# Thresholds of small scores on GpSimd, and adjacency loads behind a unit's four thresholds

## The chip, the cores and the metric

The kernel runs on one core of a Trainium2 chip. The metric is the device time of one execution in microseconds; less is better. The engines are TensorE (PE in the profile; its weight loads are PEld), VectorE (DVE), ScalarE (ACT), GpSimd (POOL) and SyncE (SP), which here only issues DMA transfers. GpSimd issues transfers too. Each engine works through its own queue in order.

## The reference

x is 4096 x 512, adj is 4096 x 4096 with entries 0 and 1. One attention layer masked by adj, and one aggregation by adj, each with a residual sum and a layer norm:

```
q, k, v = x @ Wq.T + bq, key @ Wk.T + bk, value @ Wv.T + bv
s = (q @ k.T) / 64 * adj
s = where(abs(s) < 1e-5, -1e9, s)
x = layernorm(x + (softmax(s) @ v) @ Wm.T + bm)
out = layernorm(x + relu((adj @ x) @ W.T + b))
```

## The kernel before, in words

Weights, keys and values are split into a high and a low fp16 part, and each product is made as three (high by high, low by high, high by low). After a preparation, attention runs over 64 units. A unit g is a tile of 128 rows against one half of the 4096 keys: units 0 to 31 are the tiles against the first half, units 32 to 63 against the second. NT is 32, MC is 4; b is the parity of the tile and picks the buffer.

In a unit TensorE makes the scores in four chunks of 128 x 512, each in its own PSUM bank (L887), and at the end weighs the values with the transposed probabilities (L907). The order on TensorE is scores of g, then weigh of g - 1; in the second half a product of x1 (L942) and a projection (L928) stand between them.

For each chunk c of the scores:

- VectorE masks it: prob = (score + c_now) * adj, L1559, `masked`.
- ScalarE takes its magnitude into the tile small (two buffers, c % 2), L1204. For chunk c it waits for mask c and for the sum of chunk c - 2.
- VectorE makes of it the threshold, `small_scores`, L1565: -1e9 (scaled) where the magnitude is under the limit, 0 elsewhere; `small_ready` (L1569) waits for it.
- VectorE adds the threshold to prob and keeps the maximum, `threshold`, L1572. This is called the sum below.

After the four sums come the row's maximum (L1578, L1581), the exponential on ScalarE (L1209), the high part on ScalarE (L1217) and the low part on VectorE (L1588). SP transposes both parts by DMA into PT (L387, L390), and TensorE's weigh waits for both.

The adjacency half rows come as a converting load on GpSimd's queue into adjh (two buffers, `load_adj`, L714). The load of unit g waits for all masks of unit g - 2, and for the store of that tile as bf16 (`store_adj` on SP, L374). The 64 loads stand in two loops. Behind them on the same queue stand the loads of Y, the first product of the second layer (`load_y`, L731): chunks 0 and 1 at once after the loops, chunks 4 to 6 after the last probability transpose, then 2 and 3.

SP issues in a unit, in this order: the load of t (L360), the load of x, the adjacency store, the two transposes, and then stores and transposes of other results. In the last unit it issues before the two transposes six transposes of the stored adjacency into AT (L511), for the aggregation that follows. The aggregation (L1002, L1035) starts when the last weigh, one product of x1 and one projection are done, and reads Y chunks 0 and 1 first.

Of the kernel before, what the change touches and what calls it, by code (L numbers as in the profile page):

```python
# [9 lines left out]
ALU = mybir.AluOpType  # L10
# [33 lines left out]
def attention_then_aggregation(nc, x, adj, key, value, wq, bq, wk, bk, wv, bv, wm, bm, w1, b1, out):  # L44
# [3 lines left out]
    NT = N // P  # L48
# [3 lines left out]
    MC = HALF // C  # L52
# [32 lines left out]
    with ctx:  # L85
# [17 lines left out]
        eps_s = sb(ctx, "eps_s", [P, 1], fp32)  # L103
        neg_s = sb(ctx, "neg_s", [P, 1], fp32)
# [228 lines left out]
        with nc.Block() as block:  # L333
# [327 lines left out]
            def _(pool):  # L661
# [59 lines left out]
                load_adj(1, 1, 1, 0)  # L721
                with pool.Fori(1, NT // 2) as i:
                    for b in range(2):
                        load_adj(2 * i + b, b, 2 * i + b, 0)
                with pool.Fori(0, NT // 2) as i:
                    for b in range(2):
                        load_adj(2 * i + b, b, NT + 2 * i + b, 1)

# [648 lines left out]
            def _(dve):  # L1377
# [184 lines left out]

                def small_scores(g, b, c):
                    dve.wait_ge(s_abs, MC * g + c + 1)
                    nc.vector.tensor_scalar(small[:, c % 2, :], small[:, c % 2, :], eps_s[:, 0:1], neg_s[:, 0:1],  # L1565
                                            ALU.is_lt, ALU.mult).then_inc(s_neg, 1)

                def small_ready(g, c):
                    dve.wait_ge(s_neg, MC * g + c + 1)  # L1569
# [149 lines left out]
                def score_chunks(g, b, j, n=None):  # L1719

                    def inverse(step):
                        if n is not None and step < ROOT_STEPS - 1:
                            inverse_deviation(n, 1 - b, step)

                    if not isinstance(g, int) or g != 1:
# [3 lines left out]
                        inverse(1)  # L1729
                    small_scores(g, b, 0)  # L1730
                    inverse(2)
                    small_ready(g, 0)
                    masked(g, b, 2, j)
                    inverse(3)
                    threshold(b, 0)
                    inverse(4)
                    small_scores(g, b, 1)
                    inverse(5)
                    small_ready(g, 1)
                    masked(g, b, 3, j)  # L1740
                    inverse(6)
                    threshold(b, 1)
                    inverse(7)
                    small_scores(g, b, 2)
                    inverse(8)
                    small_ready(g, 2)
                    small_scores(g, b, 3)
                    inverse(9)
# [366 lines left out]
```

## Time and profile before

| | us |
|---|---|
| three runs | 2064.64, 2064.67, 2067.79 |
| their median | 2064.67 |
| the profiled execution | 2066.32 |
| its span, first to last instruction | 2064.6 |
| TensorE busy in the span | 2036.5 |
| VectorE busy | 1446.6 |
| ScalarE busy | 698.9 |
| GpSimd busy | 81.5 |

The profile is of one execution. The span is what its rows cover; the rest of that execution's own time, 1.7 us, lies around it. TensorE's granted clock is 0.996 of full over the span. A busy time adds up the instructions of an engine; it does not say what another engine waited for. All times of rows are microseconds from the start of the span unless they are marked ns.

### The profile page before, as it was taken

The numbers are of one execution on the slowest core, as the hardware profiler recorded it, in microseconds if no ns is written. First come the engines' busy times: TensorE is split into PE (matmuls) and PEld (weight loads), VectorE is DVE, ScalarE is ACT, GpSimd is POOL, SyncE is SP. The second block draws the span as 40 slices with busy tenths as digits, with TensorE's granted clock in tenths as the row PEclk, the third lists the DMA queues.
The fourth block names the chain that finished last, engine by engine and source line by source line (L and its number), as shares of the span: only waits on it lengthen the run. The fifth ranks groups of instructions, "written<-read, shape, count | busy, mean of one in ns | idle before, by whom it ended". The sixth has DMA issues, their size and how long they took to land.

```text
span 2064.6 us, 29824 instructions
## 1 busy us (share of the span) xinstructions
PE 2036.5 (99%) x9471; PEld 977.7 (47%) x9471; DVE 1446.6 (70%) x3339; ACT 698.9 (34%) x948; POOL 81.5 (4%) x139
## 2 busy tenths in 40 slices
PE   8899999999999999999999999999999999999998
PEld 7784444444444444444444444444444444444443
DVE  4767656565656665687777777778888758877887
ACT  4665443434343434343333333334443310000000
POOL 1110000000000000000000000000000000000000
PEclk9999999999999999999999999999999999999999
DMA  7777876766677676887766666777777897555551
GB/s 260 245 275 177 207 164 165 164 171 156 169 160 172 156 172 152 219 185 163 163 163 163 163 163 163 168 173 183 182 183 210 213 276 167 125 122 124 136 133 65
DMA packets 586675, 359.58 MB, mean 174 GB/s; under 512 B 501376, under 2 KB 505472, under 8 KB 586240
## 3 DMA queue, kind: packets, MB, share of 16 engines
q1 hardware_dynamic: 565056, 275.07, 53.2%
q0 software_dynamic: 21568, 83.89, 16.8%
q8 instruction: 24, 0.39, 0.1%
q14 instruction: 27, 0.22, 0.0%
HBM read 181.15 MB, written 88.60 MB: 131 GB/s over the span
## 4 chain that ended last, share of the span: by engine, by line
PE 95%; DVE 2%; DMA 1%; ACT 1%; SPq 0%; issue 0%; ACTq 0%; DVEq 0%
PE ps L907 32%; PE ps L887 31%; PE ps L1035 16%; PE ps L928 4%; PE ps L942 4%; PE ps L836 4%; PE ps L1002 3%; PE ps L791 1%; PE ps L820 1%; PE ps L783 0%; PE ps L774 0%; DMA t_in<-t_dram 0%; DMA stg<-in_L_gnn_value 0%; DVE V L1477 0%; PE ps L861 0%
## 5 line engine op out<-in xcount | busy, mean ns | idle before, releaser
L887 PE MATMUL ps<-KT,thl 128*128 128x512 f16 x3072 | 674.9, 380 | 2.5 <-DVE thl L1529 2.5
L907 PE MATMUL ps<-V,PT 128*128 128x512 f16 x3072 | 673.5, 379 | 3.0 <-DMA PT<-Phl 2.8
L887 PEld LDWEIGHTS ps<-KT,thl 128*128 128x128 f16 x3072 | 300.9, 98 | 366.2 <-DVE thl L1529 2.7
L907 PEld LDWEIGHTS ps<-V,PT 128*128 128x128 f16 x3072 | 300.4, 98 | 365.8 <-issue 4.0
L1559 DVE SCALAR_TENSOR_TENSOR prob<-ps,c_now,adjh 128x512 f32<-128x512 f32 x256 | 191.7, 750 | 271.5 <-PE ps L887 270.3
L1204 ACT ACTIVATE small<-prob 128x512 f32<-128x512 f32 x256 | 161.1, 630 | 616.7 <-DVE prob L1559 333.4
L1588 DVE SCALAR_TENSOR_TENSOR Phl<-prob,Phl 128x2048 f16<-128x2048 f32 x64 | 146.6, 2291 | 77.1 <-ACT Phl L1217 76.8
L1572 DVE CUSTOM_DVE_ANT_0 prob<-prob,small 128x512 f32<-128x512 f32 x256 | 174.1, 682 | 0.0
L1209 ACT ACTIVATE prob<-prob,nbias,inv 128x2048 f32<-128x2048 f32 x64 | 134.0, 2094 | 94.7 <-DVE nbias L1581 94.7
L1565 DVE TENSOR_SCALAR small<-small,eps_s,neg_s 128x512 f32<-128x512 f32 x256 | 138.9, 542 | 20.7 <-ACT small L1204 20.6
L1217 ACT ACTIVATE Phl<-prob 128x2048 f16<-128x2048 f32 x64 | 122.3, 1910 | 7.1
L1369 ACT ACTIVATE p<-ps 128x512 f32<-128x512 f32 x14 | 8.4, 597 | 323.5 <-PE ps L1035 323.5
L836 PE MATMUL ps<-xT,Aq 128*128 128x512 f32 x384 | 97.6, 405 | 6.2 <-DVE xT L1381 6.2
L1035 PE MATMUL ps<-Y,AT 128*128 128x512 f16 x448 | 99.0, 379 | 0.0
L714 POOL DMA_DIRECT2D adjh<-in_adj x64 | 36.4, 569 | 1373.4 <-DMA adj_bf<-adjh 722.5
L928 PE MATMUL ps<-Wvm,UT 128*128 128x512 f16 x384 | 88.1, 379 | 0.3 <-issue 0.3
L942 PE MATMUL ps<-W1T,x1T 128*128 128x512 f16 x384 | 88.1, 379 | 0.0
L836 PEld LDWEIGHTS ps<-xT,Aq 128*128 128x128 f32 x384 | 71.6, 193 | 21.2 <-DVE xT L1381 6.9
L1035 PE MATMUL ps<-Ta,S 128*128 128x512 f16 x336 | 79.4, 379 | 0.0
L1035 PE MATMUL ps<-Tb,S 128*128 128x512 f16 x336 | 79.4, 379 | 0.0
L1035 PEld LDWEIGHTS ps<-Y,AT 128*128 128x128 bf16 x448 | 43.9, 98 | 52.8
L928 PEld LDWEIGHTS ps<-Wvm,UT 128*128 128x128 f16 x384 | 37.5, 98 | 45.8 <-DMA UT<-Uhl 0.8
(182 smaller groups left out, 1737.4 us busy)
## 6 DMA issues: line engine op xcount, KB each, us to landing
adjh<-in_adj POOLq DMA_DIRECT2D x64, 512.0 KB, 5.4
adj_bf<-adjh SPq DMA_DIRECT2D x64, 512.0 KB, 4.4
t_in<-t_dram SPq DMA_DIRECT2D x64, 256.0 KB, 2.9
x_in<-in_x SPq DMA_DIRECT2D x64, 256.0 KB, 4.2
stg<-in_L_gnn_value POOLq DMA_DIRECT2D x12, 1024.0 KB, 7.7
rows<-in_x SPq DMA_DIRECT2D x32, 256.0 KB, 5.6
t_dram<-tq POOLq DMA_DIRECT2D x8, 1024.0 KB, 9.6
o_dram<-z_out SPq DMA_DIRECT2D x32, 256.0 KB, 2.9
```

The source lines that it names most:

```text
L836: last = nc.tensor.matmul(ps[:, BT + e, :], Aq[:, m, k, e * P:(e + 1) * P], xT[:, b, s, k, :], start=(n == 0), stop=(n == 3 * KD - 1))
L887: last = nc.tensor.matmul(ps[:, BS + c, :], thl[:, b, s, k * P:(k + 1) * P], KT[:, m, k, c * C:(c + 1) * C], start=(n == 0), stop=(n == 3 ...
L907: last = nc.tensor.matmul(ps[:, BU + b, :], PT[:, b, s, m, :], V[:, v, m, :], start=(m == 0 and q == 0), stop=(m == MT - 1 and q == 2))
L928: last = nc.tensor.matmul(ps[:, BZ, :], UT[:, b, s, k, :], Wvm[:, m, k, :], start=(n == 0), stop=(n == 3 * KD - 1))
L942: last = nc.tensor.matmul(ps[:, BY, :].rearrange("p (o n) -> p o n", n=P), x1T[:, s, k, :], W1T[:, m, :, k, :], start=(q == 0), stop=(q == ...
L1035: last = nc.tensor.matmul(ps[:, bank, :].rearrange("p (s d) -> p s d", s=2), left(m), right(m), start=(m == 0), stop=(m == NP - 1))
L1204: nc.scalar.activation(small[:, c % 2, :], prob[:, b, c * C:(c + 1) * C], ACT.Abs).then_inc(s_abs, 1)
L1209: nc.scalar.activation(prob[:, b, :], prob[:, b, :], ACT.Exp, bias=nbias[:, b:b + 1], scale=inv[:, 0:1], accum_out=rsum[:, b:b + 1]).then_ ...
L1559: nc.vector.scalar_tensor_tensor(out=prob[:, b, c * C:(c + 1) * C], in0=ps[:, BS + c, :], scalar=c_now[:, b:b + 1], in1=adjh[:, b, c * C:( ...
L1565: nc.vector.tensor_scalar(small[:, c % 2, :], small[:, c % 2, :], eps_s[:, 0:1], neg_s[:, 0:1], ALU.is_lt, ALU.mult).then_inc(s_neg, 1)
L1572: nc.vector.tensor_tensor_reduce(out=prob[:, b, c * C:(c + 1) * C], in0=prob[:, b, c * C:(c + 1) * C], in1=small[:, c % 2, :], scale=1.0, ...
L1588: nc.vector.scalar_tensor_tensor(out=Phl[:, b, LO, :], in0=prob[:, b, :], scalar=P_SCALE, in1=Phl[:, b, HI, :], op0=ALU.mult, op1=ALU.subt ...
```

## The change

VectorE no longer makes the thresholds: `small_scores` is gone, and the four calls in `score_chunks` with it. `small_ready` now also waits for s_bout, a count that was reached in the preparation, and stands directly ahead of the sum of its chunk. GpSimd makes the thresholds, with the same instruction on the same tile: for a unit g, `thresholds(g)` waits four times for the scales (s_sig) and for the magnitude of a chunk. The adjacency load of unit g + 2 stands behind the four thresholds of unit g. The last two units of all have thresholds and no load behind them; the queue goes on with `load_y`.

```diff
@@ GpSimd
                 load_adj(1, 1, 1, 0)
-                with pool.Fori(1, NT // 2) as i:
+                def thresholds(g):
+                    for c in range(MC):
+                        if not isinstance(g, int):
+                            pool.to_reg(MC * g + c + 1)
+                        pool.wait_ge(s_sig, 5)
+                        pool.wait_ge(s_abs, MC * g + c + 1)
+                        nc.gpsimd.tensor_scalar(small[:, c % 2, :], small[:, c % 2, :], eps_s[:, 0:1], neg_s[:, 0:1],
+                                                ALU.is_lt, ALU.mult).then_inc(s_neg, 1)
+                pool.wait_ge(s_sig, 5)
+                with pool.Fori(0, NT // 2 - 1) as i:
                     for b in range(2):
-                        load_adj(2 * i + b, b, 2 * i + b, 0)
-                with pool.Fori(0, NT // 2) as i:
+                        thresholds(2 * i + b)
+                        load_adj(2 * i + b + 2, b, 2 * i + b + 2, 0)
+                for b in range(2):
+                    thresholds(NT - 2 + b)
+                    load_adj(b, b, NT + b, 1)
+                with pool.Fori(0, NT // 2 - 1) as i:
                     for b in range(2):
-                        load_adj(2 * i + b, b, NT + 2 * i + b, 1)
+                        thresholds(NT + 2 * i + b)
+                        load_adj(2 * i + b + 2, b, NT + 2 * i + b + 2, 1)
+                for b in range(2):
+                    thresholds(2 * NT - 2 + b)
@@ VectorE
-                def small_scores(g, b, c):
-                    dve.wait_ge(s_abs, MC * g + c + 1)
-                    nc.vector.tensor_scalar(small[:, c % 2, :], small[:, c % 2, :], eps_s[:, 0:1], neg_s[:, 0:1],
-                                            ALU.is_lt, ALU.mult).then_inc(s_neg, 1)
                 def small_ready(g, c):
+                    if not isinstance(g, int):
+                        dve.to_reg(MC * g + c + 1)
+                    dve.wait_ge(s_bout, 1)
                     dve.wait_ge(s_neg, MC * g + c + 1)
@@ VectorE, score_chunks
-                    small_scores(g, b, 0)
                     inverse(2)
-                    small_ready(g, 0)
                     masked(g, b, 2, j)
                     inverse(3)
+                    small_ready(g, 0)
                     threshold(b, 0)
                     inverse(4)
-                    small_scores(g, b, 1)
                     inverse(5)
-                    small_ready(g, 1)
                     masked(g, b, 3, j)
                     inverse(6)
+                    small_ready(g, 1)
                     threshold(b, 1)
                     inverse(7)
-                    small_scores(g, b, 2)
                     inverse(8)
                     small_ready(g, 2)
-                    small_scores(g, b, 3)
```

## Rows read from the trace of the kernel before

**Rows 1.** The page's head, and part 1: busy time and share of each engine.
```profile
span 2064.6 us, 29824 instructions
PE 2036.5 (99%) x9471; PEld 977.7 (47%) x9471; DVE 1446.6 (70%) x3339; ACT 698.9 (34%) x948; POOL 81.5 (4%) x139
```

**Rows 2.** Waits: waiter, releaser, us in total, times, longest; TensorE's and GpSimd's.
```profile
PE ps L907 <- DMA PT<-Phl: 2.8, 1, 2.8
...
POOL adjh L714 <- DMA adj_bf<-adjh: 722.5, 33, 28.6
```

**Rows 3.** The page's part 5: instructions grouped by line.
```profile
L1565 DVE TENSOR_SCALAR small<-small,eps_s,neg_s 128x512 f32<-128x512 f32 x256 | 138.9, 542 | 20.7 <-ACT small L1204 20.6
```

**Rows 4.** In order of time (start, duration, engine, line, operation): units of the first half.
```profile
805.40 0.63 ACT L1204 ACTIVATE small<-prob 128x512 f32<-128x512 f32 x1 [2.87 <-DVE prob L1559]
...
813.73 0.63 ACT L1204 ACTIVATE small<-prob 128x512 f32<-128x512 f32 x1 [1.96 <-DVE chunk_max L1572]
...
814.97 0.53 POOL L714 DMA_DIRECT2D adjh<-in_adj  x1 [21.40 <-issue]
...
815.60 0.68 DVE L1572 CUSTOM_DVE_ANT_0 prob<-prob,small 128x512 f32<-128x512 f32 x1
...
823.38 2.11 SPq L390 DMA_TRANSPOSE PT<-Phl  x1
...
832.73 10.52 PE L907 MATMUL ps<-V,PT 128*128 128x512 f16 x48
```

**Rows 5.** In order of time: a unit of the second half.
```profile
1528.58 1.91 SPq L390 DMA_TRANSPOSE PT<-Phl  x1
...
1545.08 8.15 PE L907 MATMUL ps<-V,PT 128*128 128x512 f16 x37
```

**Rows 6.** In order of time: GpSimd's own instructions at the kernel's start.
```profile
1.02 0.20 POOL L663 MEMSET ones<- 128x128 f32 x1
1.46 0.28 POOL L665 TENSOR_SCALAR_AFFINE_SELECT ident<-ident 128x128 f32<-128x128 f32 x1 [0.24 <-POOL ones L663]
```

**Rows 7.** Unit 0 in order of time, then the critical chain (start, duration, what).
```profile
174.41 1.29 ACT L1204 ACTIVATE small<-prob 128x512 f32<-128x512 f32 x2 [3.75 <-DVE prob L1559]
...
180.84 0.68 DVE L1572 CUSTOM_DVE_ANT_0 prob<-prob,small 128x512 f32<-128x512 f32 x1
...
194.48 3.11 DMA t_in<-t_dram
...
206.70 4.29 DMA PT<-Phl
```

**Rows 8.** In order of time: GpSimd's queue before the attention's end, and one transpose.
```profile
1570.55 0.53 POOL L714 DMA_DIRECT2D adjh<-in_adj  x1 [25.71 <-DMA adj_bf<-adjh]
1571.24 1.52 POOL L731 DMA_DIRECT2D Y<-y_dram  x2 [0.17 <-issue]
...
1577.44 4.23 SPq L387 DMA_TRANSPOSE PT<-Phl  x1
```

**Rows 9.** The page's part 6: issues, KB each, median us to landing.
```profile
adjh<-in_adj POOLq DMA_DIRECT2D x64, 512.0 KB, 5.4
...
PT<-Phl SPq DMA_TRANSPOSE x128, 4.5
```

**Rows 10.** In order of time: the last unit and what follows it.
```profile
1618.17 9.05 SPq L511 DMA_TRANSPOSE AT<-adj_bf  x6
...
1621.98 0.63 ACT L1204 ACTIVATE small<-prob 128x512 f32<-128x512 f32 x1 [1.90 <-DVE chunk_max L1572]
...
1631.58 2.15 SPq L390 DMA_TRANSPOSE PT<-Phl  x1
...
1636.14 10.52 PE L907 MATMUL ps<-V,PT 128*128 128x512 f16 x48 [0.25 <-issue]
...
1652.13 3.62 PE L1002 MATMUL ps<-Y,AT 128*128 128x512 f16 x16
```

**Rows 11.** Windows: busy us (count) by engine, TensorE's clock, DMA share, GB/s.
```profile
1628.00:1631.00 3.00, 3.00 (x16) 1.35 (x15) 2.90 (x5) 3.00 (x4) 0.00 (x0) 1.00 0.54 99
...
1640.00:1643.00 3.00, 3.00 (x15) 1.37 (x14) 2.09 (x9) 0.63 (x1) 0.00 (x0) 1.00 1.00 385
```

## The prediction

> **What bounds the kernel now.** I read the head of the page first, then who waited for whom on TensorE and GpSimd, then the grouped lines, then one unit of each half in order of time, then the start and the end of the attention part, where a unit has no cover. The head says that TensorE is busy for 2036.5 of 2064.6 us, VectorE for 70% and GpSimd for 4% [rows 1]. So only 28 us of the span can be gained at all, and the waits say where they lie: in the attention loops TensorE waits for a transposed probability tile once, 2.8 us [rows 2]. A unit is one row tile of one half: 48 score products of 10.52 us in all, and 48 products with the values. VectorE's threshold instruction takes 542 ns and runs 256 times, 138.9 us in all [rows 3], on an engine with room. Taking it away from VectorE therefore gains nothing by itself; what counts is whether the new path delays something that TensorE waits for.
>
> **Removed from VectorE.** Four instructions of 0.54 us a unit, 2.2 us of a unit of 21 us (first half) or 26 us (second half). Cover in the first half: the last transpose of a unit's probabilities is issued at 823.38 and takes some 4.5 us to land [rows 4, 9], so it is in at about 827.9; the product that needs it starts at 832.73 [rows 4]. That is 4.8 us of slack. In the second half the same pair is 1528.58 + 4.5 = 1533.1 against 1545.08 [rows 5], 12 us. In steady state the removal is worth 0. The four waits left on VectorE each get a second wait and register work, which lie in the same slack: 0.
>
> **Added on GpSimd: 256 thresholds.** No row shows this operation on this engine. Nearest rows: writing 128 columns takes 0.20 us, and reading and writing 128 columns 0.28 us [rows 6]. Four times these for 512 columns is 0.80 and 1.12 us, start-up counted four times. Lower end: VectorE's own 0.54 us [rows 3]. Upper end: 1.12 us plus one VectorE sum, 0.68 us [rows 4], waited out, 1.8 us. I take 0.9 us, because the two nearest rows lie around it and overstate the start-up. Each handover into GpSimd costs about 0.24 us more (the fill ends at 1.02 + 0.20 = 1.22, its reader starts at 1.46 [rows 6]), and 0.1 us back.
>
> In a steady unit the last magnitude starts at 813.73 and takes 0.63 us, and the last sum starts at 815.60 [rows 4]. After the change that sum waits for 814.36 + 0.24 + 0.9 + 0.1 = 815.60: no change. With 1.8 us it is 0.9 us late, inside 4.8 us. Only where the operation itself exceeds about 3.3 us do four of them in series (the first magnitude ends at 805.40 + 0.63 = 806.0 [rows 4], so 806.0 + 4 x 3.6 = 820.4 against 815.60) use up the 4.8 us. Cost in steady state: 0.
>
> **Unit 0 has no cover.** The row for 206.70 says that the 2.8 us of wait ends with unit 1's last transpose [rows 7]. Its chain goes back through the t_in transfer at 194.48, which SP issues only behind unit 0's transposes, and these stand behind unit 0's exponential. So whatever unit 0's last sum wins or loses reaches TensorE, up to the 2.8 us that can be won. Before, that sum starts at 180.84 [rows 7]. The two first magnitudes run from 174.41 for 1.29 us [rows 7], so the first ends at 175.05. Worked forward with 0.9 us: threshold 0 to 176.2, sum 0 to 177.0, mask 3 to 177.65, sum 1 to 178.35 (threshold 1 was ready at 177.15), magnitude 3 to 179.1, threshold 3 from 179.35 to 180.25, last sum at 180.35. That is 0.5 us earlier. With 0.54 us the same steps give 1.2 us earlier; with 1.8 us, thresholds queue on GpSimd and the last sum starts at about 182.6, 1.8 us later. **Start: -0.5 us (-1.2 to +1.8).**
>
> **Moved: the adjacency loads.** A unit's load now stands behind four thresholds instead of behind its masks. It is issued at 814.97 now and would be at about 815.6 [rows 4]; in 33 cases it waited for the adjacency store anyway [rows 2]. It takes 5.4 us [rows 9], and its unit's first mask comes some 30 us later: 0. SP's store waits for an earlier load, long landed: 0.
>
> **Moved as well, though the words do not say it: everything that stands on GpSimd's queue behind the last adjacency load.** The next instructions there are the two loads of Y, 1 MB each, issued now at 1571.24, right behind the last adjacency load at 1570.55 [rows 8]. After the change the thresholds of the last two units stand between. The last magnitude starts at 1621.98 [rows 10]; plus 0.63, 0.24 and 0.9 us the last threshold ends at about 1623.8, and the two loads are issued at about 1623.9 and 1624.7, 53 us later. Their data are needed only at 1652.13 [rows 10], so they are not late themselves. But they meet the busiest stretch of transfers: six transposes of the adjacency issued over 9 us from 1618.17 on, then the last unit's two probability transposes, the second issued at 1631.58, and the product behind them starts at 1636.14, with an idle gap before it [rows 10]. 1631.58 + 4.5 = 1636.1: this product starts the moment its transpose lands. It has no slack at all.
>
> Size: 2.1 MB at the 385 GB/s that such loads reach when alone [rows 11] is 5.4 us of all 16 DMA engines. Room for it before 1636: from 1628 to 1631 the engines are busy 0.54 of the time [rows 11], so 3 x 0.46 = 1.4 us; else they are full. The transposes end 5.4 - 1.4 = 4.0 us later. The trace has one such meeting: with the same Y loads in flight, the issue of a probability transpose at 1577.44 took 4.23 us [rows 8] against some 1.9 us else, so 2.3 us of hindrance without the adjacency transposes. Bounds: 0 (the Y data pass beside the transposes) and 7.7 us (5.4 us with no room used, plus those 2.3 us of stretched issue). I take the sum, 4.0 us, as the stretch is full. What follows on TensorE hangs on this product and shifts with it. **End: +4.0 us (0 to +7.7).** Gone from 1571 to 1581 the loads free transfers that nobody waited for: 0.
>
> **Sum:** -0.5 + 4.0 = +3.5 us. The profiled run took 2066.32 us, its span of 2064.6 and 1.7 us around it, and would become 2069.8. It lies 1.65 us over the median of the three runs; against that median of 2064.67 the forecast is 2068.2 us. Differences under 0.2%, 4.1 us, are about what a measurement of this kernel can't tell from none.
>
> **A rule against this change.** In the trace VectorE's sum takes 0.68 us alone [rows 4], and GpSimd is all but idle [rows 1], so their meeting is shown nowhere. The Trainium skill, SBUF — State Buffer, section "Who interferes with whom", says that a VectorE instruction with two SBUF inputs and a GpSimd instruction that reads SBUF block each other for the whole of the one that came first. Sum and final low part are of that kind. By that rule a threshold would sometimes wait out a sum, or a sum a threshold. No run here shows it yet.
>
> **Rivals.**
> *The end absorbs it (15%).* The transfers share the engines so that the transposes keep their pace. For it: rows with a busy share of 1.00 carry 385 GB/s, so bytes are not always what is full [rows 11]. Against it: the stretched issue at 1577.44 [rows 8]. Time: 2064.67 - 0.5 = 2064.2.
> *Blocking (12%).* Threshold and sum wait for one another. A threshold that waits out a sum is 0.9 + 0.68 = 1.6 us long, the start by the slope below +1.3, and the time 2064.67 + 1.3 + 4.0 = 2070.0. For it: both run side by side in unit 0, the one exposed place. Against it: in the worked chain most thresholds fall beside a mask, which reads PSUM. By the rule of the Trainium skill named above this is how it would come out.
> *GpSimd is dear by itself (8%), the clearest on the slower side.* Place: unit 0's chain. Price: between 0.9 and 1.8 us an operation the start goes from -0.5 to +1.8, 2.6 us for each us. With the end's 4.0 us the sum passes 4.1 us at a start of +0.1, so from 1.15 us an operation on. At 1.8 us: 2064.67 + 1.8 + 4.0 = 2070.5. Above 3.3 us the slack of the first half is gone and each of some 30 units loses four times the excess; at 4 us that is 84 us. For it: 1.12 us is the plain fourfold of the reading row [rows 6]. Against it: the fourfold counts start-up four times.
> *It gains (3%).* A gain over 4.1 us isn't there: 2.8 us is all that TensorE waits in the loops [rows 2].
> *Nothing reaches TensorE (5%).* The start's gain is lost in the transfers and the end has hidden room: 2064.7.
>
> **How the numbers follow.** The forecast, collision at the end and a cheap operation, has 57%. Its end term lies between 2 and 5.5 us, so about 0.19 of it falls over the 4.1 us and 0.38 under. Slower: 0.19 + 0.12 + 0.08 = 0.39. Within: 0.38 + 0.15 + 0.05 = 0.58. Faster: 0.03. Range: low 2064.67 - 1.2 = 2063.5; high 2064.67 + 1.8 + 7.7 = 2074.2.
>
> **What would show it.** Right: in the profile after, a new wait of some 4 us of TensorE for the last probability transpose near 1636, the Y loads issued at about 1624, and the wait of 2.8 us near 211 a little shorter; VectorE's busy time down by 139 us, GpSimd's up by about 230. Wrong: a GpSimd threshold over 1.15 us; a wait of TensorE in any other unit; no new wait near 1636; or VectorE's sums longer than 0.68 us, which would show blocking.

## The result, and the profile after

| | before | changed |
|---|---|---|
| median of the runs of this comparison, us | 2066.23 | 2084.94 |
| lowest to highest, us | 2064.64 to 2069.1 | 2082.41 to 2085.52 |
| span of the profiled execution, us | 2064.6 | 2083.8 |

The ratio is 1.0085, with a 95% interval of 1.0073 to 1.0097: the change costs 18.7 us where the forecast had +3.5. The forecast of 2068.2 us and its range to 2074.2 us were too low. The page of the changed kernel, head, part 1 and three groups of part 5 (line, engine, operation, count, then busy us and mean ns, then the idle time before them). L731 is now the threshold, L928 and L908 are TensorE's weigh and scores, L1592 is VectorE's sum, and L963 is the product of x1:

```profile
span 2083.8 us, 30506 instructions
PE 2042.5 (98%) x9471; PEld 978.7 (47%) x9471; DVE 1355.8 (65%) x3083; ACT 699.2 (34%) x948; POOL 629.2 (30%) x395
L731 POOL TENSOR_SCALAR small<-small,eps_s,neg_s 128x512 f32<-128x512 f32 x256 | 549.3, 2147 | 860.9 <-ACT small L1225 858.8
L1592 DVE CUSTOM_DVE_ANT_0 prob<-prob,small 128x512 f32<-128x512 f32 x256 | 190.0, 742 | 69.6 <-POOL small L731 69.2
L963 PE MATMUL ps<-W1T,x1T 128*128 128x512 f16 x384 | 88.1, 379 | 2.1 <-DMA x1T<-x1hl 2.1
```

The instruction that took VectorE 542 ns [rows 3] takes GpSimd 2147 ns in the mean. Its tile's view gives the spread (shortest, median, longest ns), and that of the sum:

```profile
L731 POOL TENSOR_SCALAR small<-small,eps_s,neg_s x256: 2060/2071/3187, 175.8 to 1633.3; 128x512 f32<-128x512 f32 x128
L1592 DVE CUSTOM_DVE_ANT_0 prob<-prob,small x256: 677/691/1157, 178.1 to 1636.0; 128x512 f32<-128x512 f32 x128
```

TensorE's waits in the changed kernel (us in total, times, longest), against [rows 2]; the waits of the preparation are left out:

```profile
PE ps L928 <- issue: 8.1, 3, 6.8
...
PE ps L928 <- DMA PT<-Phl: 5.1, 1, 5.1
```

Two shorter ones, for x1T (2.1 us) and for a mask (1.0 us), stand in the rows that follow. TensorE in order of time, where it loses something, and one row of the steady first half (839.45):

```profile
189.30 10.52 PE L908 MATMUL ps<-KT,thl 128*128 128x512 f16 x48 [0.97 <-DVE prob L1580]
...
215.30 13.08 PE L928 MATMUL ps<-V,PT 128*128 128x512 f16 x48 [5.12 <-DMA PT<-Phl]
...
839.45 10.52 PE L928 MATMUL ps<-V,PT 128*128 128x512 f16 x48
...
861.36 10.52 PE L928 MATMUL ps<-V,PT 128*128 128x512 f16 x48 [0.91 <-issue]
...
931.45 2.76 PE L963 MATMUL ps<-W1T,x1T 128*128 128x512 f16 x12 [2.11 <-DMA x1T<-x1hl]
...
1633.35 10.52 PE L928 MATMUL ps<-V,PT 128*128 128x512 f16 x48
...
1653.30 12.59 PE L928 MATMUL ps<-V,PT 128*128 128x512 f16 x48 [6.84 <-issue]
```

The same instructions of the kernel before are these, with those of [rows 4] and [rows 10]:

```profile
211.13 10.52 PE L907 MATMUL ps<-V,PT 128*128 128x512 f16 x48 [2.78 <-DMA PT<-Phl]
...
920.89 2.75 PE L942 MATMUL ps<-W1T,x1T 128*128 128x512 f16 x12
...
1622.78 10.52 PE L907 MATMUL ps<-V,PT 128*128 128x512 f16 x48
```

Subtracted one by one, they say where the time was lost. The scores start at 165.75 against 165.05, so 0.7 us lie ahead of the attention, in the preparation, whose length differs from run to run (the scores start between 163.78 and 165.75 in the runs read here). Then:

| stretch | how late TensorE is at its end | lost in it |
|---|---|---|
| unit 0's chain, to the weigh that starts at 215.30 (before 211.13) | 4.2 | 3.5 |
| the products behind that wait, at half clock | 6.7 | 2.5 |
| 29 units of the first half, to 839.45 (before 832.73 [rows 4]) | 6.7 | 0.0 |
| turn of the halves, to 931.45 (before 920.89) | 10.6 | 3.8 |
| the second half, to 1633.35 (before 1622.78) | 10.6 | 0.0 |
| the last weigh, 1653.30 (before 1636.14 [rows 10]) | 17.2 | 6.6 |
| the products behind that wait, at half clock | 19.2 | 2.1 |

The half clock is read in the windows: busy us and count of PE, PEld, DVE, ACT and POOL, then TensorE's granted clock, the DMA share and GB/s, behind the two waits:

```profile
215.30:216.30 1.00, 1.00 (x3) 0.40 (x4) 0.47 (x2) 0.43 (x1) 1.00 (x1) 0.50 1.01 281
220.30:221.30 1.00, 1.00 (x5) 0.44 (x4) 0.71 (x4) 0.00 (x0) 0.00 (x0) 0.89 1.01 365
...
1654.00:1655.00 1.00, 1.00 (x4) 0.34 (x3) 0.00 (x0) 0.00 (x0) 0.98 (x2) 0.50 0.57 102
```

A clock of 0.50 is the 1.2 GHz level; the 48 products that take 10.52 us at full clock take 13.08 and 12.59 us there. From 1658.00 to 1659.00 the clock is back at 1.00.

### The profile page after: what moved, and what is told of

Its sections match the earlier page's. It is cut to its first block, busy times and chain, and to the rows that moved or that the text cites. A ratio compares the mean times of both kernels' runs of the same rounds, so it can differ in the third digit from the quotient of the medians.

```text
span 2083.8 us, 30506 instructions
## 1 busy us (share of the span) xinstructions
PE 2042.5 (98%) x9471; PEld 978.7 (47%) x9471; DVE 1355.8 (65%) x3083; ACT 699.2 (34%) x948; POOL 629.2 (30%) x395
## 4 chain that ended last, share of the span: by engine, by line
PE 79%; DVE 6%; issue 3%; SPq 3%; DMA 3%; POOL 3%; ACT 2%; DVEq 0%; POOLq 0%; ACTq 0%
PE ps L928 25%; PE ps L908 24%; PE ps L1056 16%; PE ps L857 3%; PE ps L963 3%; POOL small L731 3%; PE ps L1023 3%; PE ps L949 3%; DMA stg<-in_L_gnn_value 1%; DVE Phl L1608 1%; SPq L511 1%; PE ps L812 1%; ACT prob L1230 1%; SPq L390 1%; ACT Phl L1238 1%
## 5 line engine op out<-in xcount | busy, mean ns | idle before, releaser
L731 POOL TENSOR_SCALAR small<-small,eps_s,neg_s 128x512 f32<-128x512 f32 x256 | 549.3, 2147 | 860.9 <-ACT small L1225 858.8
L928 PE MATMUL ps<-V,PT 128*128 128x512 f16 x3072 | 678.1, 381 | 13.2 <-issue 8.1
L908 PE MATMUL ps<-KT,thl 128*128 128x512 f16 x3072 | 675.0, 380 | 3.5 <-DVE thl L1550 2.5
L928 PEld LDWEIGHTS ps<-V,PT 128*128 128x128 f16 x3072 | 301.4, 98 | 380.0 <-issue 21.0
L908 PEld LDWEIGHTS ps<-KT,thl 128*128 128x128 f16 x3072 | 300.9, 98 | 367.3 <-issue 3.8
L1592 DVE CUSTOM_DVE_ANT_0 prob<-prob,small 128x512 f32<-128x512 f32 x256 | 190.0, 742 | 69.6 <-POOL small L731 69.2
L763 POOL DMA_DIRECT2D out<-y x30 | 16.2, 541 | 343.7 <-DVE y L1944 325.8
L963 PE MATMUL ps<-W1T,x1T 128*128 128x512 f16 x384 | 88.1, 379 | 2.1 <-DMA x1T<-x1hl 2.1
L963 PEld LDWEIGHTS ps<-W1T,x1T 128*128 128x128 f16 x384 | 37.5, 98 | 47.7 <-DMA x1T<-x1hl 2.6
```

The lines of the kernel that those rows point to most:

```text
L731: nc.gpsimd.tensor_scalar(small[:, c % 2, :], small[:, c % 2, :], eps_s[:, 0:1], neg_s[:, 0:1], ALU.is_lt, ALU.mult).then_inc(s_neg, 1)
L908: last = nc.tensor.matmul(ps[:, BS + c, :], thl[:, b, s, k * P:(k + 1) * P], KT[:, m, k, c * C:(c + 1) * C], start=(n == 0), stop=(n == 3 ...
L928: last = nc.tensor.matmul(ps[:, BU + b, :], PT[:, b, s, m, :], V[:, v, m, :], start=(m == 0 and q == 0), stop=(m == MT - 1 and q == 2))
L963: last = nc.tensor.matmul(ps[:, BY, :].rearrange("p (o n) -> p o n", n=P), x1T[:, s, k, :], W1T[:, m, :, k, :], start=(q == 0), stop=(q == ...
L1592: nc.vector.tensor_tensor_reduce(out=prob[:, b, c * C:(c + 1) * C], in0=prob[:, b, c * C:(c + 1) * C], in1=small[:, c % 2, :], scale=1.0, ...
```

## The experiments

The theory after the first reading had three parts: the thresholds on GpSimd are too long where a unit has no cover (its first and last units, and the turn of the halves); the Y loads meet the last transposes; and behind a long wait TensorE starts at half clock. The rivals: it is the steady units that lose; it is the order of the adjacency loads; it is the handover between engines and not the length of the operation.

Each run is set beside the kernel before as timed in the same comparison (medians of 2067.02, 2066.49 and 2066.04 us). Where a run is said to be so much under the changed kernel, two comparisons are mixed, and about 1 us of such a difference may be theirs. The diffs show the lines that matter; "..." marks what is left out.

### The order of GpSimd's queue, with either engine's thresholds

e1_y_first is the changed kernel with the Y loads back in their old place:

```diff
                         load_adj(2 * i + b + 2, b, NT + 2 * i + b + 2, 1)
-                for b in range(2):
-                    thresholds(2 * NT - 2 + b)
...
+                pool.wait_ge(w_turned, 32)
+                for c in (0, 1):
+                    load_y(c)
...
+                for b in range(2):
+                    thresholds(2 * NT - 2 + b)
...
-                pool.wait_ge(w_turned, 32)
-                for c in (0, 1):
-                    load_y(c)
```

> The changed kernel with one thing put back: the first two loads of Y stand on GpSimd's queue right behind the last adjacency load, ahead of the last two units' thresholds. Theory T (three exposed places: start, turn of the halves, end; at the end the Y loads are what collides with the transposes): the six adjacency transposes are issued in about 9 us again instead of 14.8, and of the 6.8 us wait before the last weigh only what the slower threshold chain costs is left, the 1.7 us by which the last unit's exponential is late; with it goes the 2.1 us of slower products behind the wait. Time about 6 us under the changed kernel, 2079. Rival U (the end's wait is the slow threshold chain alone): the wait stays near 6.8 us and the time at 2085.

Measured: 2076.93 us against 2067.02 (ratio 1.0053, 1.0036 to 1.0070). That is 8.0 us less than the changed kernel. The last weigh still waits, but less, and no half clock follows. The transposes of the adjacency (L511) are issued in 10.15 us here; in the changed kernel they take 14.79, from 1631.32 on, and its Y loads are issued in the middle of them (first row, of the changed kernel; the two behind it are of e1_y_first):

```profile
1635.84 1.58 POOL L752 DMA_DIRECT2D Y<-y_dram  x2
...
1628.84 10.15 SPq L511 DMA_TRANSPOSE AT<-adj_bf  x6
...
1646.58 10.52 PE L929 MATMUL ps<-V,PT 128*128 128x512 f16 x48 [2.56 <-issue]
```

e2_order_only is the kernel before with the change's order of the queue alone. VectorE makes the thresholds, and GpSimd only waits for them:

```diff
+                def thresholds(g):
+                    if not isinstance(g, int):
+                        pool.to_reg(MC * g + MC)
+                    pool.wait_ge(s_neg, MC * g + MC)
...
```

> The kernel before with thresholds on VectorE as they were; only GpSimd's queue is ordered as in the change: each adjacency load also waits until the four thresholds of the unit two before are made, and the Y loads wait for the last unit's thresholds. Theory T: the end's collision alone, some 4 to 8 us over the kernel before, 2070 to 2074, with a wait before the last weigh near 1636 and nothing new at the start or at the turn of the halves. Rival U: nothing, 2066. Rival V (the adjacency order costs in each unit): new waits inside the loops.

Measured: 2072.89 us against 2067.02 (1.0030, 1.0017 to 1.0043), 5.9 us. The last weigh waits 4.18 us and runs at half clock at first (12.93 us):

```profile
1619.01 12.65 SPq L511 DMA_TRANSPOSE AT<-adj_bf  x6
1631.77 4.49 SPq L387 DMA_TRANSPOSE PT<-Phl  x1
...
1640.89 12.93 PE L920 MATMUL ps<-V,PT 128*128 128x512 f16 x48 [4.18 <-issue]
```

The issue of the first probability transpose is stretched to 4.49 us, as the one at 1577.44 was before [rows 8]. This is the collision that the prediction worked out, with its Y loads issued at 1624.68: 3.9 us over the 0.25 of before where it had 4.0. The half clock behind it, 2.4 us, it did not have.

e2b_adj_order_only is e2_order_only without the waits for the last two units, so that the adjacency loads stand behind the thresholds and the Y loads don't:

```diff
-                for b in range(2):
-                    thresholds(2 * NT - 2 + b)
```

> As the run before, but the Y loads are free: only the adjacency loads wait for the thresholds. Theory T: no difference from the kernel before, 2066 within 2 us. Rival V: several us, growing with the number of units.

Measured: 2066.89 us against 2067.02 (1.0000, 0.9991 to 1.0010). The order of the adjacency loads costs nothing; the 5.9 us belong to the place of the Y loads alone.

### Which units lose

e3_covered_units_only leaves the thresholds of 14 units on VectorE (those at the start, at and behind the turn, two in the second half and the last two; 200 of 256 are GpSimd's), with the Y loads in front. The loops over the units are split for it, and VectorE skips the thresholds of the units in the loops:

```diff
+                def thresholds(g):
+                    if isinstance(g, int):
+                        return
...
                 def small_scores(g, b, c):
+                    if not (isinstance(g, int)):
+                        return
...
```

> GpSimd makes the thresholds of 50 units that stand inside the loops (2 to 29, 38 to 51, 54 to 61); VectorE makes those of the 14 others (0, 1, 30 to 37, 52, 53, 62, 63), in its order of before; the Y loads stand right behind the last adjacency load. Theory T (a covered unit costs nothing although one threshold takes 2.07 us): within 2 us of the kernel before, 2066, and no TensorE wait beyond those of before. Rival W (the two engines block each other in every unit, and this adds up): a good part of the 18.7 us stays.

Measured: 2066.79 us against 2067.02 (1.0002, 0.9993 to 1.0012). GpSimd's thresholds still have a median of 2071 ns here, and 50 units with them cost nothing. That settles the steady state, and with it the rival of the steady units. It changes the start, the turn and the end together; no run leaves the turn alone on VectorE.

e4_start_on_vector is the changed kernel, but units 0 and 1 have their thresholds on VectorE:

```diff
                 def thresholds(g):
+                    if isinstance(g, int) and g < 2:
+                        return
...
```

> The changed kernel, its queue order too, but VectorE makes the thresholds of units 0 and 1 as before. Theory T: the start's loss goes, which is the longer wait before the second weigh (5.1 us where before had 2.8), the new 1.0 us wait of the third unit's scores, and the 2.5 us by which the products behind the wait run slower: about 6 us under the changed kernel's 2084.9, 2079. Rival X (the start's loss is made by something else, such as the later adjacency load): no change.

Measured: 2078.10 us against 2066.49 (1.0056, 1.0039 to 1.0073), 6.8 us under the changed kernel. TensorE in order of time:

```profile
211.24 10.52 PE L939 MATMUL ps<-V,PT 128*128 128x512 f16 x48 [2.55 <-DMA PT<-Phl]
...
1647.15 11.89 PE L939 MATMUL ps<-V,PT 128*128 128x512 f16 x48 [7.50 <-issue]
```

The start is as before (2.55 us of wait, and full clock behind it), and the end is as in the changed kernel.

### The clock behind the waits

e5_filled_waits is the changed kernel with 22 and 30 products more, whose results nobody reads, in the two long waits:

```diff
                 weigh(0, 0, 0)
+                filler(BY, 22)
                 weigh(1, 1, 0)
...
+                pe.wait_ge(s_adj, MC * 2 * NT)
+                filler(BS + 1, 30)
                 weigh(2 * NT - 1, 1, NT - 1)
```

> The changed kernel with products that nobody reads: 22 ahead of the second weigh and 30 ahead of the last weigh, into banks that are free, to fill most of the two waits (4.8 of 5.1 us, 6.5 of 6.8 us). Theory C (behind a wait of some 5 us TensorE runs at half its clock for about 5 us): the waits do not shrink in sum, but the second weigh takes 10.5 us where it took 13.1, and the last 10.5 where it took 12.6, with a granted clock of 1.00 behind both: 4.6 us less, 2080. Rival D (the slow products come from contention for the on-chip memory with the transfers in flight, not from the clock): both stay slow, 2085.

Measured: 2078.99 us against 2066.49 (1.0059, 1.0042 to 1.0076). With more work the kernel is 6.0 us faster than the changed one:

```profile
214.18 10.52 PE L928 MATMUL ps<-V,PT 128*128 128x512 f16 x48 [0.42 <-DMA PT<-Phl]
...
1642.37 6.64 PE L970 MATMUL ps<-Wvm 128*128 128x512 f16 x30
...
1649.41 10.52 PE L928 MATMUL ps<-V,PT 128*128 128x512 f16 x48 [0.40 <-issue]
```

Both weighs run in 10.52 us. The table above books 4.6 us to the half clock, and these are back. The spans of the two profiled executions also differ by 6.0 us (2083.8 and 2077.8), and their rows close the sum: 1.1 us lie in the preparation (the scores start at 164.61 against 165.75), 2.5 and 2.1 us behind the two waits, and 0.2 us between. Transfers run beside both weighs here too (DMA share 0.79 and 0.54, clock 1.00 in windows of 1 us at their start). So the rival of this run, slow products by contention for the on-chip memory, falls.

### What the operation costs on GpSimd

e6_prices puts eight operations on the tile small into the preparation of the kernel before; these are four of them, each without the wait for the one ahead of it:

```diff
+                gp.tensor_copy(b, a)
+                gp.tensor_scalar(a, a, 0.5, None, ALU.mult)
+                gp.tensor_scalar(a, a, 0.5, 2.0, ALU.is_lt, ALU.mult)
+                gp.tensor_scalar(a, a, ones[:, 0:1], ones[:, 0:1], ALU.is_lt, ALU.mult)
```

> The kernel before with a row of single instructions on GpSimd while it waits for its first transfer (1.5 to 19 us), each behind the one before: fill of 128x512, copy, scale by a constant, compare and scale by constants, compare and scale by two columns (the form of the thresholds), the same on 256 columns, and a sum of two tiles. Theory P (the form itself costs 2.07 us a tile, start-up and columns): the threshold's form takes 2.0 to 2.1 us with nothing beside it, the 256 columns something over half. Rival Q (0.9 us is right for it alone, and VectorE's work beside it stretches it): about 0.9 us. The whole time is that of before, 2066, within 2 us.

Measured once, 2069.19 us. GpSimd in order of time (a copy, one multiplication by a constant, comparison and multiplication with constants, the same with columns):

```profile
2.84 0.61 POOL L680 COPY small<-small 128x512 f32<-128x512 f32 x1
3.55 1.52 POOL L681 TENSOR_SCALAR small<-small 128x512 f32<-128x512 f32 x1
5.15 2.35 POOL L682 TENSOR_SCALAR small<-small 128x512 f32<-128x512 f32 x1
7.60 2.62 POOL L683 TENSOR_SCALAR small<-small,ones 128x512 f32<-128x512 f32 x1
```

It doesn't give the price of the form alone: VectorE ran instructions with two inputs in SBUF from 5.01 us on, and the last row takes 2.62 us here and 2.07 in the loops. The same on 256 columns, with VectorE beside it too, took 2.48 us where something over half was expected. What the run does say is that a copy (0.61 us) is no measure for the others.

e7_doubled is e1_y_first with a second GpSimd operation ahead of each threshold, of the same form and size but with two multiplications by ones:

```diff
+                        nc.gpsimd.tensor_scalar(small[:, c % 2, :], small[:, c % 2, :], ones[:, 0:1], ones[:, 0:1],
+                                                ALU.mult, ALU.mult).then_inc(s_const, 1)
...
```

> The changed kernel with the Y loads in front, and before each GpSimd threshold a second instruction of the same form and size, a multiplication by one: 4.4 us a chunk instead of 2.1. It asks what a unit's delay costs once the slack is gone. In the first half the last sum comes 806.0 + 0.25 + 4 x 4.4 = 823.9 against 815.6, 8.3 us late, over a slack of 4.8 by 3.5 us. Theory T (two units are always in flight, so a unit loses half the excess): 1.75 us for each of 30 units, 52 us, and some 9 us more at the start and the end: about 2138. Rival L (the way my prediction put it, each unit loses the whole excess, or more): 2180 and above. Rival N (GpSimd's 18.2 us of work a unit fit into 20.7, so nothing is lost): about 2086. The second half, with 12 us of slack, has no new waits by T.

Measured: 2223.88 us against 2066.49 (1.0761, 1.0739 to 1.0782). The two operations side by side, and TensorE's waits:

```profile
L731 POOL TENSOR_SCALAR small<-small,ones 128x512 f32<-128x512 f32 x256 | 196.6, 768 | 770.0 <-ACT small L1232 770.0
L737 POOL TENSOR_SCALAR small<-small,eps_s,neg_s 128x512 f32<-128x512 f32 x256 | 576.4, 2251 | 44.0 <-POOL small L731 44.0
...
PE ps L970 <- DMA x1T<-x1hl: 57.9, 26, 6.7
PE ps L935 <- DMA PT<-Phl: 48.5, 28, 5.7
```

Two things follow. The same form on the same tile takes 0.77 us with two multiplications and 2.07 with the comparison. And with 3.2 us a chunk in series (the sums of one unit start 3.23 us apart) the steady units do lose: about 1.6 us each in the first half, so the cover there ends between 2.3 us (2.07 and the handover) and 3.2 us a chunk. My expected 2138 us was 86 us too low. 58 us are waits for x1T in the second half, where the theory had none: it had taken the 12 us of slack of the probability transposes [rows 5] for that of every transpose there. Another 34 us are slower products: TensorE is busy for 2070.8 us against 2036.5 before with the same 9471 products, at a mean granted clock of 0.982 against 0.996. The waits for PT came out about as expected, 48.5 us for 52.

The last four runs ask whether the comparison is the cause. e8_multiply_in_place changes one word of the changed kernel; it leaves out what a score under the limit gets:

```diff
-                                                ALU.is_lt, ALU.mult).then_inc(s_neg, 1)
+                                                ALU.mult, ALU.mult).then_inc(s_neg, 1)
```

> The changed kernel, except that each GpSimd threshold is a multiplication by eps_s and by neg_s in place of the comparison and the multiplication; the tile, the waits and the order are those of the change. What a score below the limit gets is therefore not made. Theory P, the price of the comparison is the loss: the operation takes about 0.77 us, as the added one did in the doubled kernel, and the kernel shows what the prediction worked out for 0.9 us: a wait of about 2.8 us for PT at the second unit and full clock behind it, about 4.2 us at the last weigh with full clock behind it, as with the queue order alone, 1 to 2 us at the turn of the halves and no wait for x1T. Sum about 2073 us (2071 to 2075). Rival F, the place on GpSimd is the loss (waits between engines, the shared access with VectorE), whatever the operation: over 2080 us.

Measured: 2072.45 us against 2066.04 (1.0032, 1.0021 to 1.0043). The operation's spread, TensorE's waits outside the preparation, and three of its rows:

```profile
L731 POOL TENSOR_SCALAR small<-small,eps_s,neg_s x256: 757/768/1882, 173.9 to 1621.7; 128x512 f32<-128x512 f32 x128
...
PE ps L928 <- DMA PT<-Phl: 3.0, 1, 3.0
PE ps L928 <- issue: 3.0, 1, 3.0
...
210.09 10.52 PE L928 MATMUL ps<-V,PT 128*128 128x512 f16 x48 [3.04 <-DMA PT<-Phl]
...
919.85 2.75 PE L963 MATMUL ps<-W1T,x1T 128*128 128x512 f16 x12
...
1637.89 12.21 PE L928 MATMUL ps<-V,PT 128*128 128x512 f16 x48 [3.04 <-issue]
```

All handovers, semaphore waits and queue positions are those of the change. Some 12.5 of its 18.7 us are gone with the comparison, and with them the long wait at the start, the waits at the turn of the halves and the wait for x1T. What is left is the collision at the end, as in e2_order_only (6.4 and 5.9 us by the medians). So the rival of the handover falls. One detail missed: the wait at the end was expected at 4.2 us with full clock; it was 3.04 with half clock at first (12.21 us for the 48 products, 1.7 more than at full clock).

e9_subtract_minimum makes the same threshold without a comparison. ScalarE's magnitude and eps_s are scaled by 1e14 for it, which is not shown here:

```diff
-                        nc.gpsimd.tensor_scalar(small[:, c % 2, :], small[:, c % 2, :], eps_s[:, 0:1], neg_s[:, 0:1],
-                                                ALU.is_lt, ALU.mult).then_inc(s_neg, 1)
+                        nc.gpsimd.tensor_scalar(small[:, c % 2, :], small[:, c % 2, :], eps_s[:, 0:1], 0.0,
+                                                ALU.subtract, ALU.min).then_inc(s_neg, 1)
```

> The changed kernel with the threshold worked out without a comparison: ScalarE's magnitude is scaled by 1e14, GpSimd subtracts eps_s (scaled the same) and takes the minimum with 0, which is -1e9 (scaled) at zero and 0 from the limit on. Theory P1, the comparison alone is dear on GpSimd: about 0.77 us an operation and about 2073 us, as with the multiplications. P2, everything except multiplications is dear, minimum included: about 2.07 us an operation and 2085 us. Between them the minimum costs something of its own, and the time goes with it: of the start, 4 x the excess until the half clock sets in.

Measured: 2081.72 us against 2066.04 (1.0072, 1.0057 to 1.0087); the operation has a median of 1993 ns. P1 falls, and nearly P2 holds.

e10_subtract_minimum_y_first adds the old place of the Y loads, as the diff of e1_y_first shows it.

> The kernel of e9_subtract_minimum with the loads of Y chunks 0 and 1 back ahead of the last two units' thresholds. P1: the last weigh waits under 1 us, the second unit about 2.8 us, the turn 1 us: 2067 us, within 0.2% of the kernel before. P2: 2077 us, as the comparison gave with that order. That it comes out under the kernel before by over 0.2% none of the theories expects, since TensorE's waits of before sum to a few us and none of them is one that VectorE's 139 us of thresholds caused.

Measured: 2075.01 us against 2066.04 (1.0045, 1.0031 to 1.0059), 6.7 us under e9_subtract_minimum. The price of the Y loads' place is thus seen three times: 8.0, 6.7 and 5.9 us. No version is faster than the kernel before; e2b_adj_order_only and e3_covered_units_only are level with it.

e11_four_forms gives each chunk of a unit another form, for the prices alone; none of the four makes the threshold:

```diff
+                        if c == 0:
+                            nc.gpsimd.tensor_scalar(o, i, eps_s[:, 0:1], neg_s[:, 0:1], ALU.mult, ALU.mult).then_inc(s_neg, 1)
+                        if c == 1:
+                            nc.gpsimd.tensor_scalar(o, i, eps_s[:, 0:1], 0.0, ALU.subtract, ALU.min).then_inc(s_neg, 1)
+                        if c == 2:
+                            nc.gpsimd.tensor_scalar(o, i, eps_s[:, 0:1], None, ALU.is_lt).then_inc(s_neg, 1)
+                        if c == 3:
+                            nc.gpsimd.tensor_scalar(o, i, 0.5, -3.0, ALU.is_lt, ALU.mult).then_inc(s_neg, 1)
```

> One look for prices, output not the reference's: of a unit's four GpSimd operations chunk 0 has multiply and multiply by columns, chunk 1 subtract a column and minimum with 0, chunk 2 the comparison alone with a column, chunk 3 the comparison and a multiplication with constants in place of columns. If the comparison is what is dear: 0.77, 0.77, about 2.07, about 2.07 us. If the pair of a comparison and a multiplication is: 0.77, 0.77, 0.77, 2.07. If columns as operands matter as well, chunk 3 is under 2.07. If minimum is dear too: chunk 1 about 2.07. Time between 2073 and 2085 us.

Measured once, 2076.85 us. The spreads (shortest, median, longest ns) in the order of the four forms:

```profile
L733 POOL TENSOR_SCALAR small<-small,eps_s,neg_s x64: 753/754/1871, 175.2 to 1618.8; 128x512 f32<-128x512 f32 x64
L735 POOL TENSOR_SCALAR small<-small,eps_s x64: 1997/2004/2008, 175.9 to 1621.1; 128x512 f32<-128x512 f32 x64
L737 POOL TENSOR_SCALAR small<-small,eps_s x64: 1569/1571/2123, 178.1 to 1624.5; 128x512 f32<-128x512 f32 x64
L739 POOL TENSOR_SCALAR small<-small x64: 1922/1927/2072, 180.1 to 1627.0; 128x512 f32<-128x512 f32 x64
```

Two multiplications take 0.75 us; a subtraction and a minimum 2.00; the comparison alone 1.57; the comparison and a multiplication by constants 1.93, against 2.07 with columns. So the cost isn't the comparison's alone, and columns as operands add only 0.14 us. What sets the pair of multiplications apart stays open: the single multiplication of e6_prices took 1.52 us, near the single comparison's 1.57, so a pair of multiplications by columns may be the one cheap form. No run took a single multiplication in the loops.

## Why the prediction was wrong, point by point

**VectorE's relief is worth 0:** right. Its busy time fell by 91 us and not by the 139 of the thresholds; the sums grew by 15.9 (174.1 to 190.0 us) and another small operation (rsa, L1687) by 5.4. The other 26 are overlap: the groups of VectorE's rows add up to 1583.5 us before, 137 more than its busy time, and to 1466.8 us after, 111 more, so neighbouring rows overlap and a row taken out gives back less than its length. TensorE gained nothing anywhere.

**Steady state 0:** right. The lag is 6.7 us at both ends of 29 units and 10.6 us over the second half, and e3_covered_units_only costs nothing with 200 of the 256 thresholds on GpSimd. The limit of 3.3 us an operation was too high in kind: e7_doubled loses with 0.77 + 2.25 us and one more handover, some 3.2 us a chunk.

**The price of the threshold on GpSimd, 0.9 us (0.54 to 1.8): this step failed.** It is 2.07 us. It was put at 1.8 us at most, and GpSimd's busy time at 230 us more; it rose by 548. The bound from above was made of a fill, a conditional fill and a wait [rows 6], none of which has this operation's arithmetic; e11_four_forms shows 0.75 to 2.07 us on the same tile for the same instruction with other arithmetic. With 0.77 us an operation e8_multiply_in_place gives 2072.45 us, inside the range, and its profiled execution (2069.3 us, the fastest of its runs) shows nearly what was forecast. With the start of the scores taken off (163.78 against 165.05), TensorE is 0.2 us later than before at the second unit's weigh (210.09 against 211.13), where the forecast had 0.5 us earlier, and 4.3 us later at the aggregation (1655.12 against 1652.13), where it had 3.5. Part of that match is luck: the wait at the end grew by 2.8 us and not by 4.0, and 1.7 us of half clock, which no term had, made up for it. The price is worth some 12.5 us of the 18.7, and 10.7 us lie between the changed kernel's median and the upper end of the range.

**Start, -0.5 us (-1.2 to +1.8):** it was +3.5 us, and 2.5 us of half clock behind it. Unit 0 of the changed kernel, in order of time:

```profile
175.85 8.90 POOL L731 TENSOR_SCALAR small<-small,eps_s,neg_s 128x512 f32<-128x512 f32 x4 [12.72 <-ACT small L1225]
...
182.84 1.15 DVE L1592 CUSTOM_DVE_ANT_0 prob<-prob,small 128x512 f32<-128x512 f32 x1 [2.00 <-POOL small L731]
...
184.93 0.69 DVE L1592 CUSTOM_DVE_ANT_0 prob<-prob,small 128x512 f32<-128x512 f32 x1
```

The third of the four thresholds by itself:

```profile
180.12 2.58 POOL L731 TENSOR_SCALAR small<-small,eps_s,neg_s 128x512 f32<-128x512 f32 x1
```

The four thresholds run almost without a gap, 8.90 us for four, and the last sum starts at 184.93 where it started at 180.84 [rows 7]: 3.4 us later once the 0.7 us of the preparation are off. The prediction's own slope (1.8 us later at 1.8 us, 2.6 us for each us) gives 2.5 us at 2.07, and its steps worked forward with 2.07 us give 2.8 (the first threshold from 175.29, four in series, 0.1 us to the sum: 183.67). The other 0.6 us stand in the rows: the third threshold starts together with a sum (180.12) and takes 2.58 us, 0.5 longer than 2.07, and a gap of some 0.1 us lies ahead of it, behind a magnitude that waits for the first sum. Longer sums cost no more than that gap, since the last threshold follows the third at once. e4_start_on_vector takes the whole start away, 6.8 us.

**Adjacency loads 0:** right, by e2b_adj_order_only.

**The Y loads, +4.0 us (0 to +7.7):** place and mechanism were right for the collision alone, and the size of the wait nearly (3.9 us more with VectorE's thresholds, 2.8 with the short multiplication). In the changed kernel the last weigh waits 6.6 us more, since the last unit's thresholds come late as well: its exponential starts at 1637.21 against 1624.97, 1.7 us beyond the lag of 10.6 us, and the Y loads are issued at 1635.84 and not at 1624. The two nearly add up: 2.3 us of wait from the thresholds with the Y loads in front (e1_y_first, 2.56 less 0.25) and 3.9 us from the Y loads make 6.2 of the 6.6 us. The half clock adds 2.1 us. The term was mis-sized because it was priced apart from the first one, and 1.7 to 2.3 us belong to that.

**Missing altogether:** the clock, 4.6 us by the table, and the turn of the halves, 3.8 us. Of these, 1.6 us come with short waits of two weighs (0.91 us at 861.36, 0.32 at 882.55), and 2.3 us with the product of x1, which before never waited. The rows show its chain. In the unit before it the four thresholds take 8.94 us (from 908.17), and the last sum starts at 917.29 against 901.25 before, 16.0 us later. The low part of x1 stands behind that on VectorE's queue (924.98 against 908.93, 16.1 us later), its first transpose is issued 15.9 us later (927.21 against 911.34), and the product starts 10.6 us later, since before it had room. With 0.77 us an operation, or with VectorE's thresholds in these units, it does not wait.

**The rivals.** GpSimd dear by itself had 8%, and its mark of 1.15 us is what came true, but its price stopped at 2070.5 us, since the chance was worked out on a bounded cost. Blocking is seen, and smaller than its rival had it. The changed kernel, where the last threshold and a sum of the last unit start together:

```profile
1633.25 0.69 DVE L1592 CUSTOM_DVE_ANT_0 prob<-prob,small 128x512 f32<-128x512 f32 x1 [0.70 <-POOL small L731]
1633.31 2.58 POOL L731 TENSOR_SCALAR small<-small,eps_s,neg_s 128x512 f32<-128x512 f32 x1 [0.20 <-ACT small L1225]
...
815.34 2.07 POOL L731 TENSOR_SCALAR small<-small,eps_s,neg_s 128x512 f32<-128x512 f32 x1 [0.34 <-ACT small L1225]
817.01 0.68 DVE L1592 CUSTOM_DVE_ANT_0 prob<-prob,small 128x512 f32<-128x512 f32 x1
```

The threshold that begins 0.06 us behind the sum is 0.51 us longer. The sum at 182.84, which begins 0.16 us behind a threshold (182.68), takes 1.15 us, 0.47 longer, and does not wait for the threshold's end at 184.75. And the sum at 817.01 runs inside a threshold (815.34 to 817.41) and takes its usual 0.68 us. The Trainium skill, SBUF — State Buffer, section "Who interferes with whom", has the first instruction hold the other off for its whole length; this trace roughly agrees for a threshold behind a sum (0.51 us of the 0.63 that the sum still had to run), and not for a sum behind or inside a threshold.

## What to carry to other kernels

An engine's price for an instruction has to come from a row with the same arithmetic, not only the same shape; where there is none, the upper bound is open, and a forecast that hangs on it should run it to several times the nearest row. Work moved to an idle engine costs nothing where a unit has cover (and gained nothing here, as VectorE bound nothing), and costs where it has none: price the first unit, the last one and each seam between loops by themselves, and move only the covered units. And an instruction put into a queue moves all that stands behind it there, here two loads for 5.9 to 8.0 us.

## What the runs showed that I had not expected

- On GpSimd, 128 x 512 in fp32: two multiplications by columns 0.77 us, comparison and multiplication by columns 2.07, with constants 1.93, comparison alone 1.57, subtraction and minimum 1.99 to 2.00. VectorE does the threshold in 0.54 us [rows 3]. No run varied the values that the comparison reads.
- At a weigh, TensorE came back at 1.2 GHz behind waits of 5.12 and 6.84 us (changed kernel), 4.92 (e1_y_first), 4.18 (e2_order_only), 7.50 (e4_start_on_vector), 3.16 (e6_prices), 5.25 and 8.42 (e9_subtract_minimum), 4.60 (e10_subtract_minimum_y_first), 4.75 and 4.73 (e11_four_forms) and once of 3.04 us (e8_multiply_in_place, the end). It came back at full clock behind 2.78 us (before), 2.55, 2.56, 2.91 (e2b_adj_order_only) and another one of 3.04 us (e8_multiply_in_place, the start). The 48 products took 11.89 to 13.39 us in place of 10.52, so it cost 1.4 to 2.9 us each time, and a wait filled with unread products brought no such loss.
- VectorE's sum takes 1.15 us instead of 0.68 where it starts 0.16 us behind a GpSimd threshold (182.84), 0.71 where it starts together with one (180.12, and then the threshold is the longer), and 0.68 where it falls inside one (817.01).
